# Second feed-forward over 28 blocks of 128 rows instead of 32 of 112, its norm moved into the attention

## The reference

```python
x = x + xattn0(layernorm(x), ctx)         # one head
x = x + ffn0(layernorm(x))                # three low-rank-adapted blocks
x = x + xattn1(ctx, layernorm(x))         # 16 heads
x = x + ffn1(layernorm(x))                # the stage that is changed

def rmsnorm(x, w):        return x * rsqrt(mean(x*x) + 1e-8) * w
def activation_quant(x):                  # one scale per row
    s = 127 / clip(max|x|, 1e-5);  return clip(round(x*s), -128, 127) / s
def weight_quant(w):                      # ternary, one scale per matrix
    s = 1 / clip(mean|w|, 1e-5);   return clip(round(w*s), -1, 1) / s
def bitlinear(x, nw, w):  return activation_quant(rmsnorm(x, nw)) @ weight_quant(w).T
def ffn1(x):                              # 256 -> 1024 -> 256
    h = bitlinear(x, norm1_w, w1)
    h = act_scale * relu(h)**2 + act_bias
    return bitlinear(h, norm2_w, w2)
```

## Time and profile before

| | before |
|---|---|
| median of 3 runs | 1348.44 us (1347.06 to 1351.72) |
| profiled execution | 1348.56 us, its span 1346.8 us |
| busy share of the span | PE 84%, PEld 60%, DVE 70%, ACT 43%, POOL 33% |
| attention (stage 3), first to last copy of its weighed values | 749.4 to 1109.8 us |
| first and last activation of stage 4 | 1134.0 and 1331.4 us |
| granted TensorE clock, whole span | 0.916 of full speed |

### The profile page before, as it was taken

The page is one execution under the profiler, slowest core; times in us unless marked ns, Lnnn a source line. Parts: engine busy times, 40 slices in busy tenths (PEclk is TensorE's granted clock), DMA queues, the critical chain, the costliest instruction groups (busy, mean ns, idle before and its releaser), DMA issues. The chain is left out here.

```text
span 1346.8 us, 30729 instructions
## 1 busy us (share of the span) xinstructions
PE 1124.6 (84%) x9322; PEld 804.9 (60%) x9322; DVE 943.1 (70%) x2495; ACT 583.5 (43%) x1009; POOL 442.6 (33%) x792
## 2 busy tenths in 40 slices
PE   3699999999996989898784899999999983676765
PEld 2577777777775666665441666666666661554544
DVE  2646665655564676766654788888888864999997
ACT  1323222222232111211151555565556663888886
POOL 0324444444441222212104122322222224545451
PEclk7699999999998999999895999999999995778777
DMA  9323333333321000000058766666666610000000
GB/s 210 109 58 87 86 86 92 94 93 91 86 86 34 1 1 0 0 0 1 1 109 159 143 129 128 127 133 130 128 128 129 135 25 19 14 20 17 17 17 25
DMA packets 105310, 99.26 MB, mean 74 GB/s; under 512 B 43923, under 2 KB 98742, under 8 KB 105270
## 3 DMA queue, kind: packets, MB, share of 16 engines
q1 hardware_dynamic: 105270, 98.76, 31.9%
HBM read 70.76 MB, written 27.61 MB: 73 GB/s over the span
## 5 line engine op out<-in xcount | busy, mean ns | idle before, releaser
L1190 DVE TENSOR_REDUCE nm<-bank 112x1 f32<-112x375 f32 x512 | 257.7, 539 | 54.3 <-PE bank L1645 53.4
L864 ACT ACTIVATE pT<-bank 125x448 f32<-125x448 f32 x384 | 191.4, 541 | 111.9 <-PE bank L1675 77.5
L1645 PE MATMUL bank<-ks,qs 96*128 96x375 bf16 x512 | 162.1, 338 | 18.3 <-POOL qs L681 17.1
L1661 PE MATMUL bank<-qs,ks 128*128 128x112 bf16 x1536 | 140.8, 215 | 21.9 <-DMA qs<-mrow 21.9
L1661 PEld LDWEIGHTS bank<-qs,ks 128*128 128x128 bf16 x1536 | 103.0, 99 | 57.6 <-issue 42.2
L1675 PE MATMUL bank<-pT,vaug 125*32 125x112 f32 x3072 | 113.6, 266 | 0.0
L815 ACT ACTIVATE yT<-bank,bcol,gcol 128x448 f32<-128x448 f32 x48 | 32.1, 720 | 160.0 <-PE bank L1545 160.0
L1563 PE MATMUL bank<-wffT,hT 128*112 128x256 f32 x384 | 98.5, 390 | 0.0
L1675 PEld LDWEIGHTS bank<-pT,vaug 125*32 125x32 f32 x3072 | 67.3, 109 | 41.0 <-issue 28.3
L1405 PE MATMUL bank<-wv1T,ctxT 128*125 128x256 f32 x384 | 88.0, 379 | 0.0
L1405 PE MATMUL bank<-ctxT,wk1T 128*128 128x375 f32 x256 | 86.0, 478 | 0.0
(11 more groups left out here) (210 smaller groups left out, 2440.0 us busy)
## 6 DMA issues: line engine op xcount, KB each, us to landing
k_parts_dram<-kp SPq DMA_DIRECT2D x192, 93.8 KB, 3.6
ks<-k_parts_dram SPq DMA_DIRECT2D x64, 281.2 KB, 4.2
cnat<-in_ctx_dram SPq DMA_DIRECT2D x32, 375.0 KB
ks<-k_parts_dram SPq DMA_DIRECT2D x64, 187.5 KB, 3.9
ks<-k_parts_dram SPq DMA_DIRECT2D x64, 93.8 KB, 3.2
q_parts_dram<-qp SPq DMA_DIRECT2D x48, 112.0 KB, 2.2
qs<-q_parts_dram SPq DMA_DIRECT2D x64, 84.0 KB, 4.0
x_stream<-in_x_dram SPq DMA_DIRECT2D x4, 896.0 KB, 14.7
```

The costliest lines, as they stand in the source:

```text
L864: act.activation(pT[:, u % 4, :], B3[u % 3][0:TP], ACT.Exp).then_inc(probs_made, 1)
L1190: dve.tensor_reduce(nm[:, h:h + 1], A3[h % 3][0:L], AX_X, ALU.max, negate=True).then_inc(head_max_taken, 1)
L1645: mm(A3[h % 3], qs[par][0:KS, h * L:h * L + P], ks[par][0:KS, h * T:(h + 1) * T], start=True, stop=True).then_inc(max_scores_made, 1)
L1661: last = mm(B3[c][:, j * L:(j + 1) * L], ks[par][:, h * T + c * TP:h * T + c * TP + P], qs[par][:, h * L:(h + 1) * L], start=True, stop=True)
```

## The change

Stage 4 works on 28 blocks of 128 rows. For this the rows of `x`, and of the normed `y`, are written to memory in attention and read back in the new cut, 7 blocks (896 rows) a DMA. The norm of the rows moves to GpSimd inside attention; the product with `norm2_w` moves from VectorE to GpSimd; rounding of the hidden row moves from ScalarE to VectorE; the two clips go; output uses two banks; `activate` comes first in VectorE's step. The barrier between stages 3 and 4 goes: the first blocks' work is written into the end of attention. The ternary weights are stored to memory after setup and loaded again at attention's end, into the region where the values lie (`v_all`).

```diff
 # SyncE, start of stage 1
+            sp.dma_start(wd[0], w1T...); sp.dma_start(wd[1], w2T...)       # 512 KB each
 # SyncE, attention
+            def store_x(b):    # waits x_after_attn2(b), and x_stored(b-1)
+            def store_y(b):    # waits y_made(b)
+            def load_y(c, stored):
+                sp.wait_ge(y_stored, 16 * stored)
+                if c >= 1:
+                    sp.wait_ge(y_tiles_in, 16 * c)
+                sp.dma_start(yt4[:, c * CH:(c + 1) * CH, :], tiles_of(yd, c)).then_inc(y_tiles_in, 16)
@@ def moves(b, par), after the second load_half
+                if not isinstance(b, int) or b >= 2:
+                    store_y(b - 2)
+                if not isinstance(b, int) or b >= 1:
+                    store_x(b - 1)
+                if isinstance(b, int) and b >= B - 3:
+                    load_y(b - (B - 3), b - 1)
+                if isinstance(b, int) and b == B - 2:
+                    sp.wait_ge(ffn2_weights_in, 16)
+                    everywhere_late(n2_bc, L1_ffn_norm2_w, HID)
+                    sp.dma_start(w1T4..., wd[0]).then_inc(ffn2_weights_in, 16)
+                    sp.dma_start(w2T4..., wd[1]).then_inc(ffn2_weights_in, 16)
 ...
-            stage_end(sp, "sp", 4)
+            store_y(B - 2)
+            store_x(B - 1)
+            sp.wait_ge(values_weighed, 12 * B)
+            sp.wait_ge(x_stored, 16 * B)
+            for c in range(NCH):
+                sp.dma_start(xt4[:, c * CH:(c + 1) * CH, :], tiles_of(xd, c)).then_inc(x_tiles_in, 16)
+            store_y(B - 1)
+            load_y(NCH - 1, B)
 # GpSimd, attention: after factors4(b) (two more one-column operations)
+            def norm_y(b):
+                pool.wait_ge(x_stored, 16 * (b + 1))
+                pool.tensor_tensor(x_row, x_row, rs4[:, row(b)].broadcast_to([L, D]), ALU.mult)
+                pool.tensor_tensor(x_row, x_row, rr4[:, row(b)].broadcast_to([L, D]), ALU.subtract)
+                pool.tensor_tensor(x_row, x_row, n1_bc[0:L, :], ALU.mult).then_inc(y_made, 1)
 # GpSimd, feed-forward
+            def step4(i, par, n):
+                weigh_h(i, par)   # waits activation_made(i); gh = th * n2_bc, 128 x 1024
+                root_h(i, par)    # waits square_sum_made(i); two one-column operations
 # ScalarE
             over_thirds(act, step3)
             pv_out(B - 1)
+            xq_out(0, 0)
             o_out(B - 1)
-            stage_end(act, "act", 4)
+            def step4(i, par, n):
+                hq_out(i - 2)
+                xq_out(i + 2, par)       # waits x_int_turned(i+2)
+                squares(i, par)
+                relu(i + 1, 1 - par)
+                square(i + 1, 1 - par)
+            relu(0, 0); xq_out(1, 1); square(0, 0)
 # VectorE
             over_thirds(dve, step3)
+            dve.wait_ge(y_tiles_in, 16)   # then max_x, factor_x, inverse_x, round_x of blocks 0 and 1
             norm_o(B - 1) ... keep4(B - 1)
-            stage_end(dve, "dve", 4)
+            def step4(i, par, n):
+                activate(i, par)          # waits squares_made(i), that is square(i)
+                round_x(i + 2, par)
+                result(i - 3, 1 - par, n - 2 + par)
+                max_h(i - 1, 1 - par)     # waits hidden_weighted(i-1)
+                factor_h(i - 1, 1 - par)
+                max_x(i + 3, 1 - par)
+                inverse_h(i - 1); scale_h(i - 1); out_factor(i - 1)
+                round_h(i - 1, 1 - par)   # 128 x 1024
+                factor_x(i + 3); inverse_x(i + 3)
+            # before step 2: y_tiles_in of 3 chunks; before step 3: x_tiles_in of all 4
 # TensorE
+            pe.wait_ge(ffn2_weights_in, 64)
+            in_turn(0, 0)
+            in_product(0, 0)
             fin_turn(B - 1)
             fin_project(B - 1)
-            stage_end(pe, "pe", 4)
+            pe.wait_ge(x_after_attn2, B)
+            in_turn(1, 1)
+            in_product(1, 1)
+            def step4(i, par, n):
+                out_turn(i - 2, par)      # waits hidden_rounded(i-2)
+                in_turn(i + 2, par)       # waits x_rounded(i+2)
+                out_product(i - 2, par)   # waits hidden_intT_ready(i-2)
+                in_product(i + 2, par)    # waits x_intT_ready(i+2)
```

More of the change, by code:

```diff
@@ L386, in over_thirds, with over_tiles @@
                 step(b, b % 3, b // 3)
+        def over_tiles(eng, step, head, tail):
+            for i in range(head):
+                step(i, i % 2, i // 2)
+            with eng.Fori(0, (NT - head - tail) // 2) as i:
+                step(2 * i + head, 0, i + head // 2)
+                step(2 * i + head + 1, 1, i + head // 2)
+            for i in range(NT - tail, NT):
+                step(i, i % 2, i // 2)
         block = ctx.enter_context(nc.Block())
@@ L1259, in _ @@
+            over_thirds(dve, step3)
+            dve.wait_ge(ffn2_constants_made, 3)
+            dve.wait_ge(y_tiles_in, 16)
+            for i in range(2):
+                max_x(i, i)
+                factor_x(i, i)
+                inverse_x(i, i)
+                round_x(i, i)
             norm_o(B - 1)
@@ L1367, in _ @@
-            for b in range(2):
-                max_x(b, b)
-                factor_x(b, b)
-                factors_x(b, b)
-                round_x(b, b)
-                clip_x(b)
-            for b in range(4):
-                step4(b, b % 2, b // 2)
-            with dve.Fori(0, (B - 6) // 2) as i:
+            max_x(2, 0)
+            factor_x(2, 0)
+            inverse_x(2, 0)
+            late = CH * (NCH - 1) - 3
+            assert late % 2 == 0
+            for i in range(4):
+                if i == 2:
+                    dve.wait_ge(y_tiles_in, 16 * (NCH - 1))
+                if i == 3:
+                    dve.wait_ge(x_tiles_in, 16 * NCH)
+                step4(i, i % 2, i // 2)
@@ L1387, in _ @@
+            for i in range(NT - 4, NT + 3):
+                step4(i, i % 2, i // 2)
         @block.tensor
@@ L1732, in _, with in_turn, in_product @@
                 scores_for_max(1, 1, 0, h)
+            def in_turn(i, par):
+                pe.wait_ge(x_rounded, i + 1)
+                if not isinstance(i, int) or i >= 2:
+                    pe.wait_ge(relu_made, i - 1)
+                for k in range(KC):
+                    last = pe.transpose(XT4[par][:, k, :], xq4[par][:, k * P:(k + 1) * P], ident[:, :])
+                last.then_inc(x_int_turned, 1)
+            def in_product(i, par):
+                pe.wait_ge(x_intT_ready, i + 1)
+                for half in range(2):
+                    last = over_rows(H4[par][:, half * 512:(half + 1) * 512], lambda k: xqT[:, k, :],
+                                     lambda k: w1T4[:, k, half * 512:(half + 1) * 512])
+                last.then_inc(hidden_made, 1)
@@ new lines, in out_turn, with out_product @@
+            def out_turn(i, par):
+                pe.wait_ge(hidden_rounded, i + 1)
+                for c in range(HC):
+                    last = pe.transpose(HT4[:, c // 4, (c % 4) * P:(c % 4 + 1) * P], hq4[par][:, c * P:(c + 1) * P], ident[:, :])
+                last.then_inc(hidden_int_turned, 1)
+            def out_product(i, par):
+                pe.wait_ge(hidden_intT_ready, i + 1)
+                if not isinstance(i, int) or i >= 2:
+                    pe.wait_ge(result_made, i - 1)
+                for c in range(HC):
+                    last = mm(Y4[par], hqT[:, c, :], w2T4[:, c, :], start=(c == 0), stop=(c == HC - 1))
+                last.then_inc(ffn2_out_made, 1)
```

493 lines of the change are left out of this document (237 added, 256 removed).

## The result

The changed kernel takes 1329.35 us (median of 4 runs, 1326.86 to 1330.85) against 1349.57 (4 runs, 1347.06 to 1351.72): a ratio of 0.9849, 95% interval 0.9825 to 0.9873. It is 20 us faster. 1302 was forecast: 46 faster than the 1348.44 known then. The profiled execution took 1329.82 us, its span is 1328.0.

A forecast was written before the change was run, and what follows sets the result against it. VectorE bounds stage 4, TensorE attention; the changed stage 4 is set by a ring. Step 3 at 1143, plus 24 x 5.85 (140.4), tail 14.5, attention 2 and 1.8 from span to time: 1302 us, range 1284 to 1330.

The forecast's parts named there:

- Attention: In attention, GpSimd's added work and the stores fit into gaps; 2 us taken, bounds 0 and 0.7 us a step.
- The leading case: Whole forecast: stage 4 at 5.6 to 6.2 us a step, 1290 to 1314 in all; chance 0.52.
- The new step: VectorE's own work in one stage 4 step after the change: 4.8 us, not the period.
- The ring: Stage 4 period: loop from square through activate, round_x, in_turn, xq_out, squares and relu back to square, 5.4 us at full clock.
- TensorE's level: Stage 4: a step is 6.7 us at TensorE's lower level, 5.4 at the upper; 5.85 taken.
- faster ring: Stage 4 rival: TensorE mostly at the upper level, 5.4 us a step, 11 less, 1291; chance 0.15.
- GpSimd's product: Stage 4: the 1024-column product on GpSimd takes 2.3 us, bounds 1.95 and 2.9, and is hidden.
- The port: Stage 4 rival: weigh_h gets in front of round_x behind each activation, 2.5 us a step, total 1357; chance 0.08.
- The hand-over: Attention to stage 4: weights loaded by 1115.5, first activation near 1123.5, 10.5 us earlier than before.
- The wait for x rows before step 3: Early stage 4: VectorE waits for x rows read until 1143, where the period would reach step 3 at 1141.
- The tail: End of stage 4, from last activation to the span's end: 14.5 us, before 15.4.
- Start to attention: From the start to the first copy of weighed values: 749.4 us, the same as before.

The follow-up runs named there:

- e1_no_norm: The changed kernel with the three 256-column GpSimd operations of norm_y made one-column ones, all stores, loads and semaphores kept: 1293.61 us, ratio 0.9578.
- e6_round_first: e2_x_early with round_x(i+2) put ahead of activate(i) in VectorE's stage 4 step, nothing left out: 1278.53 us, ratio 0.9461.
- e2_x_early: The changed kernel with the store of residual rows issued right behind the minus-max rows instead of behind the second half's loads: 1290.65 us, ratio 0.9566.

## Why the prediction was wrong

**The step that failed** is "Attention": "GpSimd gets two one-column operations and three of 256 columns, 0.2 to 0.7 each: about 3 us more of a step of 11.6 us", bounds 0 and 0.7, 2 us taken in all. GpSimd's work was costed as filling its idle time, and the only harm weighed was a late DMA. Measured are 38.1 us more than before, 36.1 more than forecast, 1.2 a block, and the mechanism is the very one that the prediction had read in the earlier trace rows and priced for stage 4: GpSimd and VectorE hold each other up. It was never laid against attention's VectorE list, where the casts stand on the way to TensorE's next block. "`lay_v` is queued behind them, but its values are read two steps later" was right on the reader and missed the rest: e1_no_norm shows that `lay_v` in a new place costs 10 us with no norm at all. And the bound of 0.7 came from the stores' gap alone; a bound for three operations that meet `parts_m` was to be had: 722 ns each by the earlier trace rows make 2.2 us a block, above what was paid. That 1329.35 still lies inside the range of 1284 to 1330 is luck: the range gave attention 22 us, it lost 38, and a faster stage 4 made up for it. The leading case asked for 5.6 to 6.2 a step and 1290 to 1314 in all, and neither came.

The Trainium skill ("SBUF — State Buffer", section on its two separate sides) lists which VectorE operations take the port pair shared with GpSimd: those in a mode that uses two ports, and those with two inputs in SBUF against a GpSimd operation that reads SBUF; the other side blocks for the whole instruction. The runs agree: casts and `tensor_tensor` stretch from 0.17 to as much as 1.45 us, `scalar_tensor_tensor` to 1.51, reductions stay at 0.17. (No row names an operation's mode.) The prediction had cited this rule, for one pair of operations of stage 4.

**The new step** of 4.8 us for VectorE: 5.47 less the wait of 0.73 is 4.74. Right. **The ring**, 5.4 at full clock: 5.47 in the timeline, VectorE's wait in front of each activation, and e6_round_first, which takes `round_x` out of it, has shorter steps. Right.

**TensorE's level** was over-weighted: 5.85 a step was taken, a mixture of 5.4 and 6.7. Windows of 5.5 us, each a step long:

```profile
1209.84:1215.34 5.50, 3.29 (x23) 2.20 (x22) 4.56 (x13) 4.69 (x6) 3.62 (x3) 1.00 0.07 24
1215.31:1220.81 5.50, 4.38 (x22) 2.83 (x22) 4.51 (x12) 4.69 (x6) 3.57 (x3) 0.69 0.07 24
1220.87:1226.37 5.50, 3.67 (x25) 2.23 (x23) 4.56 (x13) 4.69 (x6) 3.62 (x3) 1.00 0.07 24
```

Of 21 such windows 14 are at 0.99 or 1.00 and 7 at 0.69; none is wholly at the lower level, and the one at 0.69 holds a step of 5.56 beside one of 5.47. (The first three steps, ahead of these windows, are at 0.50 throughout and took 19.1 us, where the forecast has 19.5.) So the mixture of whole steps at 6.7 was the term that was mis-sized: the seven with a part at the lower level take 5.47 to 5.72. Against the earlier trace rows with 0.76, the stretch is at 0.85. The case "faster ring" was what happened: the 25 steps behind the first two took 137 us, 5.48 each. The mean of all 27, 5.57, holds a second step of 7.8: the activation there is held for 2.91 us behind GpSimd's first product, late because it is queued behind the last block's norm.

**GpSimd's product** was taken at 2.3 and measured 2.34 to 2.41. **The port** in the steady step: `round_x` takes 0.34 to 0.36 in all 28 steps. Right.

**The hand-over.** TensorE waited for the weights until 1154.39, 3.4 us after the last copy, where 5.7 was reckoned (1115.5 less 1109.8), and the first activation came 11.6 after the copy against 13.7. The wait for x rows before step 3 did not show: that activation waits 0.80 us for ScalarE's square and for no DMA. Both reads were shorter than reckoned: the weights' group, first issue to last landing, took 11.0 us (1143.2 to 1154.2) for 13.5, the x rows 13.2 (1162.6 to 1175.8) for 19.2. The 207 GB/s was read where the DMAs were full, but from 1168.2 to 1176.0, at a DMA share of 0.99, they moved 314. The 1.5 of latency in both terms stands in no row. **The tail**: 15.0 for 14.5.

**Start to attention**, +3.1: in the eight experiments, with the same code up to there but for the order of later work, the first copy lies between 746.9 and 753.7. It is no effect of the change that one execution could show.

Without the collision, in e2_x_early, the five stretches of the first table are 752.2, 362.0, 11.0, 149.6 and 14.2: 10.9 below the forecast's span, nearly all of it the faster ring (10.3) and the hand-over (2.7), less the later start. The other mechanisms of the forecast hold, and the one left out took 39 of 59 us back (1329.35 against 1290.65).

## What to carry to other kernels

Work given to an idle engine costs nothing only where its operations don't meet those of an engine that it shares a port with: lay the list of either engine's operations against the other's by time, the short ones too, and ask which DMA or semaphore fixes the meeting. A held operation has no idle time before it, so views of waits don't show it: compare a line's mean with its least. A wait in front of moved work also moves everything queued behind it. If two such lists meet, shift one (here one DMA issue moved up by seven places is worth 39 us) or write the short one as a form that doesn't share.

## What was not expected of the hardware

A VectorE operation that waits for GpSimd can be passed over when the next GpSimd operation follows back to back: it waited for two in a row (1.44 us for 16 columns, 3.47 for 1024). It is not always so. In the changed kernel an operation that waited at the end of L766 was held on through L728 in 23 of 24 blocks, and one that waited at the end of L728 was let through before L732, just as close behind, in 26 of 26. What decides is not shown. A gap of 0.18 us, where GpSimd waited for its own semaphore, let one of 0.17 through. A reduction over an axis of one element writes the bf16 cast in 0.170 us and was never held: 169 to 171 ns in 32 blocks each of two, GpSimd at work in 53 of these 64 cases.
